# Silu on ScalarE in place of tanh and a gating instruction on VectorE, in a linear-attention and FP4 feed-forward block

## What is computed

```
xn  = layernorm(x)
# attention: 16 heads of 16 channels, buckets of 64 tokens
q, k, v = split(xn @ W_qkv.T);  q = softmax(q) / 4;  k = exp(k)
context, k_sum = sums of k*v and k over all earlier buckets
attn = (q @ context) / max(q @ k_sum, 1e-6);   a = attn @ W_out.T
# feed-forward: each linear quantises both operands to FP4 in blocks of 16
gate = fp4_linear(xn, w_gate);   up = fp4_linear(xn, w_up)      # 704 wide
h    = silu(gate) * up
out  = x + a + fp4_linear(h, w_down)
```

## Time and the profile before

| | |
|---|---|
| median of 3 runs | 1552.2 us (1551.77 to 1552.58) |
| the profiled execution | 1554.58 us, its span 1552.8 us |
| ScalarE busy | 771.6 us (50%) |
| VectorE busy | 1498.1 us (96%) |
| TensorE busy (matmul records) | 1385.2 us (89%) |

### The profile page before, as it was taken

One profiled execution on the slowest core, in us unless ns is written; L12 is line 12 of the kernel. 1 busy time (PEld: TensorE's weight loads), 2 busy tenths in 40 slices (PEclk: granted clock), 3 DMA queues, 4 the chain that ended last, 5 costly groups with the idle time before them and its releaser, 6 DMA issues.

```text
span 1552.8 us, 42501 instructions
## 1 busy us (share of the span) xinstructions
PE 1385.2 (89%) x10702; PEld 949.7 (61%) x10702; DVE 1498.1 (96%) x5042; ACT 771.6 (50%) x2072; POOL 173.2 (11%) x541
## 2 busy tenths in 40 slices
PE   0169999999999999999999999999999999999996
PEld 0146666666666666666666666666666666666664
DVE  5859999999999999999999999999999999999996
ACT  1775445555454544455454545454554545454541
POOL 1521010101001010101001010101010010101000
PEclk9969999999999999999999999999999999999998
DMA  5003233332333333333323333332333232323223
GB/s 110 4 8 66 58 63 66 71 69 55 78 67 68 62 75 68 61 69 68 72 55 78 65 65 65 74 68 58 71 66 77 52 78 65 66 63 75 62 50 70
DMA packets 293240, 100.00 MB, mean 64 GB/s; under 512 B 258272, under 2 KB 292704, under 8 KB 293216
## 3 DMA queue, kind: packets, MB, share of 16 engines
q1 hardware_dynamic: 293216, 99.73, 30.7%
HBM read 19.99 MB, written 16.78 MB: 24 GB/s over the span
## 4 chain that ended last, share of the span: by engine, by line
DVE 54%; issue 34%; DVEq 7%; ACT 2%; PE 1%; SPq 1%; DMA 0%; POOL 0%; ACTq 0%; POOLq 0%
DVE q_rows L858 4%; DVE osum L895 4%; DVE hw L820 4%; DVE xblk L753 3%; DVE h L739 3%; DVE drec L713 2%; DVE xw L838 2%; DVE hv L802 2%; DVE hq L830 2%; DVE xq_s L871 2%; DVE hu L824 2%; DVE c_row L883 1%; DVE xblk L772 1%; DVE att L718 1%; DVE qsh L681 1%
## 5 line engine op out<-in xcount | busy, mean ns | idle before, releaser
L550 ACT ACTIVATE att_t<-trp 128x256 f16<-128x256 f32 x256 | 98.1, 383 | 357.7 <-PE trp L1105 353.2
L1150 PE MATMUL outp<-w_down_cat,q_rows 128*128 128x256 f16 x1408 | 247.0, 274 | 0.0
L534 ACT ACTIVATE qexp<-qsh,c_q 128x256 f32<-128x256 f32 x128 | 65.0, 508 | 226.5 <-DVE qsh L681 226.5
L398 POOL TENSOR_TENSOR var_scaled<-squares,var_mul 128x1 f32<-128x1 f32 x128 | 24.5, 192 | 1246.8 <-ACT scratch L488 1239.8
L1150 PEld LDWEIGHTS outp<-w_down_cat,q_rows 128*128 128x128 f16 x1408 | 138.7, 98 | 16.7
L1152 PE MATMUL outp<-w_down_lo,q_rows 128*128 128x256 f16 x640 | 148.4, 275 | 0.0
L513 ACT ACTIVATE xnt<-trp 128x256 f16<-128x256 f32 x256 | 96.6, 377 | 57.4 <-PE trp L1045 57.4
L746 DVE TENSOR_REDUCE hblk<-h 128x44 f32<-128x704 f32 x128 | 123.9, 968 | 0.1
L802 DVE TENSOR_TENSOR hv<-h,hblk 128x704 f32<-128x704 f32 x128 | 112.8, 881 | 0.0
L1019 PE MATMUL unit1a<-w_gate,xqt 128*128 128x352 f16 x256 | 80.5, 314 | 32.9 <-DVE qsh L681 31.5
L1019 PE MATMUL unit0a<-w_gate,xqt 128*128 128x352 f16 x256 | 80.5, 314 | 32.4 <-DVE qsh L681 31.5
(11 more groups left out here) (213 smaller groups left out, 4399.5 us busy)
## 6 DMA issues: line engine op xcount, KB each, us to landing
xring<-x SPq DMA_DIRECT2D x128, 128.0 KB, 2.7
out<-xring SPq DMA_DIRECT2D x128, 128.0 KB, 2.5
xqt<-xq_s SPq DMA_TRANSPOSE x128, 2.4
q_rows<-q_rows SPq DMA_TRANSPOSE x128, 3.5
raw_qkv<-wqkv_t SPq DMA_DIRECT2D x1, 768.0 KB, 7.8
raw_gate<-wgate SPq DMA_DIRECT2D x8, 88.0 KB
raw_up<-wup SPq DMA_DIRECT2D x8, 88.0 KB
raw_down<-wdown SPq DMA_DIRECT2D x1, 704.0 KB, 6.3
```

The source lines that it names most:

```text
L550: nc.scalar.activation(att_t[:, par, part, :], tr32, ACT.Copy).then_inc(att_split, 1)
L1150: nc.tensor.matmul(downp, hqt[:, par, m, :], w_down_cat[:, m, :], start=(m == 0), stop=False)
```

## The change

ScalarE evaluates Silu of the gate half in place of tanh, with a scale that is twice the old one, since tanh took half the argument. VectorE's `gate_h` goes, two instructions in a step; `times_up` multiplies ScalarE's result `sg` with the up half and waits for `silu_done`. The two factors of the rounding, `c_d` and `h_floor`, are taken from a new `c_u`. The semaphores `tanh_done` and `ga_done` become one.

```diff
-            def tanh_gate(t, half, par):
+            def silu_gate(t, half, par):
                 if not is_tile(t):
                     return
                 act.wait_ge(gu_done, after(t, 2, half + 1))
                 if begun(t - 1):
-                    act.wait_ge(ga_done, after(t - 1, 2, half + 1))
-                nc.scalar.activation(th[:, half, :], unit[(par + half) % 2][0][:, 0:FH], ACT.Tanh, scale=c_g[:, :])\
-                    .then_inc(tanh_done, 1)
+                    act.wait_ge(h_done, after(t - 1, 2, half + 1))
+                nc.scalar.activation(sg[:, half, :], unit[(par + half) % 2][0][:, 0:FH], ACT.Silu, scale=c_g[:, :])\
+                    .then_inc(silu_done, 1)
...
-            def gate_h(t, half, par):
-                if not is_tile(t):
-                    return
-                dve.wait_ge(tanh_done, after(t, 2, half + 1))
-                if begun(t - 1):
-                    dve.wait_ge(h_done, after(t - 1, 2, half + 1))
-                nc.vector.scalar_tensor_tensor(ga[:, half, :], th[:, half, :], 1.0,
-                                               unit[(par + half) % 2][0][:, 0:FH], ALU.add, ALU.mult)\
-                    .then_inc(ga_done, 1)
-
             def times_up(t, half, par):
                 if not is_tile(t):
                     return
-                dve.wait_ge(ga_done, after(t, 2, half + 1))
+                dve.wait_ge(silu_done, after(t, 2, half + 1))
                 if begun(t - 2):
                     dve.wait_ge(hq_step, after(t - 2, 14, 8))
-                nc.vector.tensor_tensor(h[:, par, half * FH:(half + 1) * FH], ga[:, half, :],
+                nc.vector.tensor_tensor(h[:, par, half * FH:(half + 1) * FH], sg[:, half, :],
                                         unit[(par + half) % 2][1][:, 0:FH], ALU.mult).then_inc(h_done, 1)
...
-            nc.vector.tensor_scalar(c_g[:, :], pow2[:, 2:3], XS ** -1 * 2.0 ** -12 * UNTIE, None, ALU.mult).then_inc(factors, 1)
+            nc.vector.tensor_scalar(c_g[:, :], pow2[:, 2:3], XS ** -1 * 2.0 ** -11 * UNTIE, None, ALU.mult).then_inc(factors, 1)
```

More of the change, by code:

```diff
@@ L103, in linear_attention_fp4_ffn_block @@
         c_d = sb("c_d", [P, 1])
-        c_gu = sb("c_gu", [P, 1])
+        c_u = sb("c_u", [P, 1])
         h_floor = sb("h_floor", [P, 1])
@@ L146, in linear_attention_fp4_ffn_block @@
         xqt = sb("xqt", [P, 2, 2, D], fp16)
-        th = sb("th", [P, 2, FH])
-        ga = sb("ga", [P, 2, FH])
+        sg = sb("sg", [P, 2, FH])
         h = sb("h", [P, 2, F])
@@ L216, in linear_attention_fp4_ffn_block @@
         gu_done = sem("gu_done")
-        tanh_done = sem("tanh_done")
-        ga_done = sem("ga_done")
+        silu_done = sem("silu_done")
         h_done = sem("h_done")
@@ L566, in step @@
                 exp_q(k + 1, odd)
-                tanh_gate(k, 0, par)
+                silu_gate(k, 0, par)
                 split_xnt(k + 2, par, 0)
@@ L571, in step @@
                 split_xnt(k + 2, par, 1)
-                tanh_gate(k, 1, par)
+                silu_gate(k, 1, par)
                 normalise(n, d + 3)
@@ L917, in step @@
                 round_h(k - 1, 2)
-                gate_h(k, 0, par)
                 row_factor(k - 1, odd)
@@ L929, in step @@
                 attention(k, par, 2)
-                gate_h(k, 1, par)
                 attention(k, par, 3)
@@ L966, in _ @@
             nc.vector.tensor_scalar(c_q[:, :], pow2[:, 0:1], XS ** -1 * 2.0 ** -14, None, ALU.mult).then_inc(factors, 1)
-            nc.vector.tensor_scalar(c_g[:, :], pow2[:, 2:3], XS ** -1 * 2.0 ** -12 * UNTIE, None, ALU.mult).then_inc(factors, 1)
+            nc.vector.tensor_scalar(c_g[:, :], pow2[:, 2:3], XS ** -1 * 2.0 ** -11 * UNTIE, None, ALU.mult).then_inc(factors, 1)
             nc.vector.tensor_scalar(c_o[:, :], pow2[:, 0:1], pow2[:, 1:2], 2.0 ** -20, ALU.mult, ALU.mult).then_inc(factors, 1)
-            nc.vector.tensor_scalar(c_gu[:, :], pow2[:, 2:3], pow2[:, 3:4], 2.0 ** -44 * UNTIE ** 2, ALU.mult, ALU.mult).then_inc(factors, 1)
+            nc.vector.tensor_scalar(c_u[:, :], pow2[:, 3:4], 2.0 ** -21 * UNTIE, None, ALU.mult).then_inc(factors, 1)
             dve.wait_ge(factors, 7)
             nc.vector.tensor_scalar(wscale[:, :], wscale[:, :], 2.0 ** 14, None, ALU.mult).then_inc(factors, 1)
-            nc.vector.tensor_scalar(c_d[:, :], c_gu[:, :], pow2[:, 4:5], 2.0 ** -1 * UNTIE, ALU.mult, ALU.mult).then_inc(factors, 1)
-            nc.vector.reciprocal(h_floor[:, :], c_gu[:, :]).then_inc(factors, 1)
+            nc.vector.tensor_scalar(c_d[:, :], c_u[:, :], pow2[:, 4:5], 2.0 ** -1 * UNTIE, ALU.mult, ALU.mult).then_inc(factors, 1)
+            nc.vector.reciprocal(h_floor[:, :], c_u[:, :]).then_inc(factors, 1)
             dve.wait_ge(factors, 10)
```

## The result

The changed kernel takes 1670.6 us, median of 4 runs (1668.5 to 1672.4), where the kernel before took 1552.0 beside it: ratio 1.076, 95% interval 1.074 to 1.078, slower. The forecast was 1657, range 1604 to 1730. The profiled execution took 1672.38 us.

A forecast was written before the change was run, and what follows sets the result against it. VectorE bounds the kernel at 11.235 us a step; a 9.31 us chain plus two loads (2.76) was to make it 12.07. Times 124 steps, +103.5, with edges +105 on the profiled execution, median 1657 us, range 1604 to 1730.

The forecast's parts named there:

- Which chain: Closed loop through TensorE and ScalarE, less_xn to next less_xn, 9.31 us without loads; both table loads make it the longest.
- The forecast that `qsh` is in time: VectorE's qsh is ready before ScalarE reaches qexp, with 1.8 us of slack, so ScalarE does not wait.
- The length of it: Step of the closed chain: 9.31 us plus two table loads, 2.76 us, giving 12.07 us against 11.235 before.
- start and end of the run, put at +1.2: A further 10.9 us step after the 124 also holds both loads, adding 1.2 us; the first tile's load is hidden.
- A load was priced 1.38: Each ScalarE table load costs its 1.28 us record plus 0.10 of lost overlap on the chain.
- The rival of a price far above the record: A table switch on ScalarE costs 2.57 us, making the step 14.44 and the time 1950 us; chance 0.12.
- the lower bound of a load that overlaps its neighbours: A ScalarE load overlaps like an ordinary instruction, 1.18 us each; step 11.67, time 1606 us.
- the 72 that I read from TensorE's busy share: Without other changes the step stops at TensorE's own work, 10.66 us, gaining 0.58 us a step.
- The rival "faster, since the loads hide": One ScalarE load stays off the chain, leaving 10.69 us; TensorE's work sets the pace, 1484 us; chance 0.05.
- the rival, at 0.03: TensorE's clock falls for good, the dense 5.91 us piece about doubles and the time passes 2200 us; chance 0.03.

The follow-up runs named there:

- the kernel with the waits swapped: Changed kernel plus a one-column exponential at step end, drawing its load into ScalarE's idle place, and the Silu's two waits swapped: 1494.4 us, ratio 0.963.
- the swap alone: Changed kernel with only the Silu's waits for gu_done and h_done swapped, both loads left in place: 1670.3 us, ratio 1.077.

## Why the prediction was right, and where its numbers were off

**Which chain.** Right. The changed kernel's step is `less_xn`, the dense TensorE piece, `att_t`, the load, the keys' copies, `qexp`, the load, the Silu, `xnt`. Taking the loads away (1467), moving one of them (1545, 1494) and adding two (2.92 us on ScalarE's piece) each changed the time through this chain, and giving VectorE 0.82 us more left the step as it was. The forecast that `qsh` is in time held too: ScalarE waits for it once.

**The length of it.** 12.07 was forecast, 12.196 measured; times 124 that is 15.6 us. The median was off by 13.6. The difference is in the edges: start and end of the run, put at +1.2, gave 117.8 - 119.1 = -1.3, which takes off 2.5, and the median lies 1.8 below the profiled execution and not 2.4, which adds 0.6. The step itself was sized too small in three places. A load was priced 1.38; from start to start the two add 0.40 + 1.30 - 0.28 = 1.42 and 0.52 + 1.29 - 0.41 = 1.40, together 0.06 more. The rows of the chain around them are 0.03 longer in sum, `kexp` to `vaug` and the Silu to `xnt` by 0.02 each (Silu has 554 ns against tanh's 544). And the 0.42 us from the transpose of `att` to `att_t` is that of one kind of step only: in the other the changed kernel has 706.54 - 706.04 = 0.50 (rows below), so steps of 12.24 and 12.16 alternate. I read the chain off one step of a loop whose body has two. The two stretches at the lower clock and shorter steps at the start are in the mean of 124 steps as well and nearly cancel.

```profile
706.04 0.38 PE L1091 MATMUL trp<-ident,att 128*128 128x128 f32 x2
```

```profile
706.54 0.38 ACT L548 ACTIVATE att_t<-trp 128x256 f16<-128x256 f32 x1 [2.84 <-PE trp L1091]
```

**The price of a load.** The load begins 0.02 us after the instruction ahead has ended (722.36 behind 721.84 + 0.50), and the Silu 0.01 after the load. The rival of a price far above the record falls, and so does the lower bound of a load that overlaps its neighbours. By the Trainium skill, "ScalarE: Activation LUTs", section "What ACT_TABLE_LOAD costs", a switch is 2.66 us with 1380 ns of draining; the rows here give 1.41 on the path at both places, and the measurement decides.

**Where the expected gain went.** Without loads, the lost gating gives 85 us, not the 72 that I read from TensorE's busy share. With them it gives nothing in the step and about 4 us in all, since the chain through both doesn't pass VectorE's gating.

**The rival "faster, since the loads hide"** did not come true in the change and was made true by an experiment: its 10.69 us a step is near the 10.77 of the kernel with the waits swapped, 1494 us where the rival had 1484. Its condition, one load in ScalarE's first idle place, was right, and lacked a second one: the other load must not stand behind a wait for gate and up.

**TensorE's clock** was not where the forecast left it. The sum had no term for it, and the rival, at 0.03, spoke of a fall for good. In the profiled execution of the change it fell for 3.4 us twice in the loop, some 3 us in all; in that of the swap alone, with the same step, it did not fall in the loop, and that one took 1670.4 us where the changed kernel's took 1672.4. It did fall in every step when the idle time was 4.07 us. So the mechanism exists, and in the change it is worth a few us at most.

## What to carry to other kernels

Before a function on ScalarE is swapped for another, read the compiled order for table loads, and ask of each load not whether the engine has room but what closed chain of the loop passes its place: a busy share of 50% did not help. A load can be drawn into idle time by a one-column activation of the coming function, and the activation's own wait must not be queued ahead of the load. What VectorE gave back by losing an instruction was that one's start-to-start time, less what it had covered between a writer and its reader. And read two steps where the loop's body has two.

## What I had not expected of the hardware

- TensorE's granted clock fell to 0.50, the 1.2 GHz level, behind 4.07 us of idle time that recurred in each step of 17 us, and was back at 1.00 within the step; with 1.14 us of idle time in each 12.2 it stayed at 1.00 but for two stretches of 3.4 us in the loop. So 2.92 us more on ScalarE cost 4.9 a step.
- A VectorE instruction that reads what the one ahead wrote, and waits for its semaphore, started 0.11 us later than an unrelated one in two places: `drec` to `att` 0.27 against `drec` to `ga` 0.16, `xw` to `xu` 0.31 against `xw` to `h` 0.20.
- All 254 loads of the changed kernel, the one at its start with them, had the same 1283 ns, to the exponential's table and to the Silu's.
